# Two of the scan's output additions move from VectorE to ScalarE and TensorE, and the sixteen carry copies of a chunk from GpSimd to ScalarE

## What is computed

```python
dA  = exp(delta[..., None] * A)                   # A: 512 x 16
dBu = (delta * u)[..., None] * B[:, :, None, :]
def step(h, inp):                                 # along the 4096 tokens
    h = dA_t * h + dBu_t
    y_t = einsum('bdn,bn->bd', h, C_t)            # the sum over the 16 states
y = (y + D_skip * u) * silu(z)
out = y @ W_out
```

## Time and profile before

| | |
|---|---|
| median of 3 runs | 2296.16 us (2295.28 to 2297.36) |
| the profiled execution's own time | 2299.68 us |
| its span, first to last instruction | 2297.6 us |
| mean granted TensorE clock | 0.956 of full speed |
| busy: DVE, POOL, PE, ACT | 2096.4, 2039.3, 2053.2, 1696.3 us |
| starts of scan 0 of chunks 7 and 8 | 986.20 and 1121.90 us |

### The profile page before, as it was taken

How to read it: one execution, slowest core, us unless ns; L and a number is a source line. 1 busy time by engine, 2 the same in 40 slices (tenths; PEclk the granted TensorE clock), 3 DMA queues, 4 the chain that set the end, 5 groups by cost and what they waited for, 6 DMA issues and landing times. The chain is left out here.

```text
span 2297.6 us, 30579 instructions
## 1 busy us (share of the span) xinstructions
PE 2053.2 (89%) x9280; PEld 1333.5 (58%) x9280; DVE 2096.4 (91%) x2960; ACT 1696.3 (74%) x2584; POOL 2039.3 (89%) x1657
## 2 busy tenths in 40 slices
PE   7669989899998999999899999999899899987968
PEld 4346565655566565665656556565566656555554
DVE  4999999999999999999999999999999999998940
ACT  5657878787788777787778787878778787875732
POOL 4777999989999998999999999999999999898944
PEclk8759999999999999999999999999999999998989
DMA  5111211112122111112111211211112121111201
GB/s 146 33 33 48 74 56 60 61 52 60 56 68 60 54 61 60 56 56 65 59 58 51 66 60 57 65 60 56 51 60 71 56 61 51 55 58 47 74 19 46
DMA packets 92995, 134.28 MB, mean 58 GB/s; under 512 B 12048, under 2 KB 43024, under 8 KB 92832
## 3 DMA queue, kind: packets, MB, share of 16 engines
q1 hardware_dynamic: 92832, 132.34, 18.6%
HBM read 123.13 MB, written 9.18 MB: 58 GB/s over the span
## 5 line engine op out<-in xcount | busy, mean ns | idle before, releaser
L915 DVE TENSOR_TENSOR_SCAN h<-d_a,carry,d_bu 128x512 f32<-128x512 f32 x1024 | 1258.5, 1268 | 73.4 <-ACT d_a L678 47.0
L1203 POOL TENSOR_TENSOR d_bu<-delta_u,b_rows 128x1024 f32<-128x1024 f32 x512 | 1203.0, 2362 | 4.7 <-issue 0.6
L678 ACT ACTIVATE d_a<-delta,a_neg 128x512 f32<-128x512 f32 x1024 | 694.0, 689 | 425.9 <-DVE h L915 421.3
L495 PE MATMUL ht<-ident,h 128*128 128x128 f32 x4096 | 598.1, 288 | 114.8 <-DVE y_t L930 72.5
L495 PEld LDWEIGHTS ht<-ident,h 128*128 128x128 f32 x4096 | 490.3, 147 | 337.4 <-issue 113.0
L930 DVE SCALAR_TENSOR_TENSOR y_t<-ht,c_t,y_t 128x512 f32<-128x512 f32 x800 | 555.6, 736 | 8.7 <-PE ht L495 8.2
L578 PE MATMUL ring<-x_t,w_gate_sb 128*128 128x512 f32 x640 | 312.1, 617 | 12.8 <-ACT delta L877 10.2
L607 PE MATMUL dn<-w_down_sb,up_hidden 128*128 128x256 f32 x1280 | 305.5, 382 | 6.9 <-ACT c_t L882 4.1
L585 PE MATMUL ring<-x_t,w_up_sb 128*128 128x512 f32 x640 | 294.5, 603 | 16.0 <-ACT silu_gate L809 15.5
L607 PEld LDWEIGHTS dn<-w_down_sb,up_hidden 128*128 128x128 f32 x1280 | 234.6, 190 | 64.3 <-issue 32.5
L1265 POOL TENSOR_TENSOR up_hidden<-silu_gate,up_hidden 128x512 f32<-128x512 f32 x160 | 204.6, 1279 | 51.2 <-ACT up_hidden L815 35.0
(11 more groups left out here) (136 smaller groups left out, 2177.4 us busy)
## 6 DMA issues: line engine op xcount, KB each, us to landing
b_rows<-b_rows_hbm SPq DMA_DIRECT2D x256, 256.0 KB, 3.5
coef_rows<-coef_rows_hbm SPq DMA_DIRECT2D x128, 256.0 KB, 3.4
xa<-L_attn_x_in SPq DMA_DIRECT2D x16, 512.0 KB, 5.0
xr<-L_attn_x_in SPq DMA_DIRECT2D x16, 512.0 KB, 5.0
out<-xr SPq DMA_DIRECT2D x15, 512.0 KB, 2.9
w_in_sb<-L_attn_W_in_in SPq DMA_DIRECT2D x1, 1024.0 KB, 6.3
w_gate_sb<-L_ffn_experts_gate_in SPq DMA_DIRECT2D x2, 512.0 KB, 4.8
w_up_sb<-L_ffn_experts_up_in SPq DMA_DIRECT2D x2, 512.0 KB, 5.5
```

What stands on the lines that cost most here:

```text
L495: last = nc.tensor.transpose(HT[q % HTS][:, j * P:(j + 1) * P], H[:, (NS * c + n) % HS, j, a * P:(a + 1) * P], IDN[:, :])
L678: nc.scalar.activation(DA[i % DAS][:, :], DL[:, r, j, :], ACT.Exp, scale=ANEG[:, j, n:n + 1]).then_inc(ex.sem, 1)
L915: nc.vector.tensor_tensor_scan(H[:, (NS * s + n) % HS, j, :], DA[(n * J + j) % DAS][:, :], BU[:, (2 * n + j // 2) % 4, j % 2, :], CARRY[:, ...
L1203: nc.gpsimd.tensor_tensor(BU[:, (2 * n + h) % 4, :, :], DU[:, 2 * h:2 * h + 2, :], BB[:, n % 2, :].unsqueeze(1).to_broadcast([P, 2, T]), A ...
```

## The change

The pair of slot 46 (q = 40 and 41, quarters 0 and 1 of state 10) is no longer added by DVE. ACT copies it, times C, into `YD[:, 0]` and `YD[:, 1]`, and PE turns it onto y's banks at the chunk's end as it does the held pair: four transposes in slot 63, four in slot 1. All 16 `keep_state` copies of a chunk go from POOL to ACT, at slots written out in `KEEP_ACT` and `KEEP_LAST`, each ahead of that slot's `decay`. `skip_u` is one slot later.

```diff
+        y_kept = [stage(f"y_kept{i}", 2) for i in range(1)]
-        scan, add_c, carry = ..., stage("add_c", (NS - 2) * NT - 6), ...
+        scan, add_c, carry = ..., stage("add_c", (NS - 2) * NT - 8), ...
-        YD_DVE, Y_GATE, OUT_PE = (3, 3, 4, 4), 4, (5, 5, 6, 6)
+        YD_DVE, Y_GATE, OUT_PE = (4, 4, 5, 5), 4, (5, 5, 6, 6)
+        KEEP_ACT = {5: (0,), 12: (1,), 13: (2,), 18: (3,), 20: (4,), 26: (5,), 31: (6,), 37: (7, 8), 41: (9,),
+                    47: (10,), 49: (11,), 59: (12, 13), 63: (14,)}
+        KEEP_LAST = 5
-        SIDE_SLOT, NEXT_SLOT, HELD_SLOT = 20, 26, 56
+        SIDE_SLOT, NEXT_SLOT, HELD_SLOT, YD_SLOTS = 20, 26, 56, (46,)
+        YD_Q = [ADDS[t] for t in YD_SLOTS]
+        ELSEWHERE = SIDE_Q + NEXT_Q + HELD_Q + tuple(q for pair in YD_Q for q in pair)
...
                             if t == 1 and i == 1:
                                 transpose_held(s - 1, (2, 3))
+                                transpose_kept(s - 1, (2, 3))
...
                     if with_scan and t == SLOTS - 1:
                         transpose_y(s, lo, (0, 1), (0, 1))
                         transpose_held(s, (0, 1))
+                        transpose_kept(s, (0, 1))
...
+            def transpose_kept(c, js):
+
+                for i, pair in enumerate(YD_Q):
+                    pe.wait_ge(y_kept[i].sem, y_kept[i].at(c))
+                    for q in pair:
+                        a = q % NT
+                        for j in js:
+                            nc.tensor.matmul(yd_bank(j)[:, a * P:(a + 1) * P],
+                                             YD[:, 2 * i + q - pair[0], j * P:(j + 1) * P], IDN[:, :],
+                                             start=False, stop=False, is_transpose=True, skip_group_check=True)
...
+            def keep_state(c, r, n):
+
+                act.wait_ge(scan.sem, scan.at(c, (n + 1) * J))
+                nc.scalar.activation(CARRY[:, r, n, :], H[:, (NS * c + n) % HS, :, T - 1], ACT.Copy)\
+                  .then_inc(carry.sem, 1)
+
+            def kept_state(c, r, i, q, prepared):
+
+                n, a = q // NT, q % NT
+                act.wait_ge(ht_full.sem, ht_full.at(c, q + 1))
+                act.wait_ge(o_full.sem, o_full.at(c - 1))
+                act.wait_ge(conv_last.sem, conv_last.at(prepared))
+                nc.scalar.activation(YD[:, 2 * i + q - YD_Q[i][0], :], HT[q % HTS][:, :], ACT.Copy,
+                                     scale=CT[:, r, a, n:n + 1]).then_inc(y_kept[i].sem, 1)
...
+                    if ffn and t == KEEP_LAST:
+                        keep_state(s - 1, o, NS - 1)
+                    if with_scan:
+                        for n in KEEP_ACT.get(t, ()):
+                            keep_state(s, r, n)
...
+                    for i, pair in enumerate(YD_Q):
+                        if with_scan and t == YD_SLOTS[i]:
+                            for q in pair:
+                                kept_state(s, r, i, q, s + 1 if prep else s)
...
-                    if t > 0 and t % NT == 0 and with_scan:
-                        keep_state(s, r, n - 1)
...
-                    if t == 0 and ffn:
-                        keep_state(s - 1, o, NS - 1)
...
-            def keep_state(c, r, n):
-
-                pool.wait_ge(scan.sem, scan.at(c, (n + 1) * J))
-                nc.gpsimd.tensor_tensor(CARRY[:, r, n, :], H[:, (NS * c + n) % HS, :, T - 1],
-                                        ONE[:, 0:1].to_broadcast([P, J]), ALU.mult).then_inc(carry.sem, 1)
```

More of the change, by code:

```diff
@@ L167, in mamba_moe_kernel @@
         y_held = stage("y_held", 2)
+        y_kept = [stage(f"y_kept{i}", 2) for i in range(1)]
         stream, tail = stage("stream", 1), stage("tail", NT)
-        scan, add_c, carry = stage("scan", NS * J), stage("add_c", (NS - 2) * NT - 6), stage("carry_s", NS)
+        scan, add_c, carry = stage("scan", NS * J), stage("add_c", (NS - 2) * NT - 8), stage("carry_s", NS)
         stats = {w: stage(f"stats_{w}_s", 2 * NT) for w in ("xa", "o", "x1", "y")}
@@ L239, in added @@
                 return y_held.sem, y_held.at(c, q - HELD_Q[0] + 1)
-            return add_c.sem, add_c.at(c, q - NT + 1 - 2 * ((q > SIDE_Q[1]) + (q > NEXT_Q[1]) + (q > HELD_Q[1])))
+            for i, pair in enumerate(YD_Q):
+                if q in pair:
+                    return y_kept[i].sem, y_kept[i].at(c, q - pair[0] + 1)
+            return add_c.sem, add_c.at(c, q - NT + 1 - sum(q > other for other in ELSEWHERE))
         def gate_slot(f):
@@ L928, in add_state @@
                 else:
-                    dve.wait_ge(*added(c, q - NT if q - NT not in HELD_Q else q - 2 * NT))
+                    apart = q - NT in HELD_Q or any(q - NT in pair for pair in YD_Q)
+                    dve.wait_ge(*added(c, q - 2 * NT if apart else q - NT))
                 nc.vector.scalar_tensor_tensor(YT[:, a, :], HT[q % HTS][:, :], CT[:, r, a, n:n + 1],
@@ L979, in body @@
                     for q in ADDS.get(t, ()):
-                        if with_scan and q >= NT and q not in SIDE_Q + NEXT_Q + HELD_Q:
+                        if with_scan and q >= NT and q not in ELSEWHERE:
                             add_state(s, r, q)
```

## The result

The changed kernel takes 2284.47 us (median of 5, 2284.43 to 2286.68) against 2295.92; the ratio is 0.995 (95% interval 0.9939 to 0.9961). The forecast was 2284.5, range 2272 to 2295. The profiled execution took 2284.43 us, its span 2282.4, so it stands at its median, while the one of before stood 3.5 us above its own.

A forecast was written before the change was run, and what follows sets the result against it. POOL, gapless from slot 45, was taken to set scan 60's start, not the busier DVE. 0.35 - 0.06 + 0.46 + 0 = 0.75 us a steady chunk, 11.7 in all, against the median 2296.16: 2284.5 us, range 2272 to 2295.

The forecast's parts named there:

- POOL, not DVE, sets scan 60: POOL's gapless run from slot 45 sets scan 60's start; 0.61 us gained there out of 1.30 + 0.37.
- the third copy: Slot 56's carry copy: its 0.15 us doesn't help slot 60's additions, so 0.46 remain.
- Chunk 0: No experts there and POOL has room, so DVE's 1.30 us counts whole.
- Scan 42: Three copies (slots 28, 32, 36) leave POOL's run ahead of its d_bu, 0.45 us; its whole 0.35 wait goes.
- A small ACT copy costs 0.06 us: Each of 16 carry copies takes 0.06 us of ACT, bounds 0 and 0.16; only slot 26's lies on a chain.
- The boundary at 0: From one chunk's end to the next, with four transposes before the last state's: net 0, bounds -0.3 and +0.3 us.
- The later skip_u costs 0 and returns 0.15: skip_u one slot later: x_in's delay is covered, cost 0; DVE's idle of 0.15 us ahead of it returns.
- The tail, 0.86: After the last chunk, the eight transposes lie in the open chain and cost 0.86 us.
- The sum: 0.75 us a steady chunk, 14 of them 10.5; 11.7 altogether, 2288.0 from the profiled execution, 2284.5 from the median.
- the first (DVE's time kept whole): POOL gives way more than counted, DVE takes its 1.30 us whole: 24 us, so 2272; chance 0.16.
- the second (the boundary takes it back): Transposes and slot 63's copy hold scans 2 and 3; only scan 42's 0.29 stays: 2291 us; chance 0.20.
- the third: PE's clock drops in slots 4 to 9 behind a larger gap ahead of x_in: slower, up to 2304; chance 0.12.

The follow-up runs named there:

- half_block9: The change with POOL's second product of expert block 9 cut to 4 columns, one routed expert left unweighted; 2267.36 us, ratio 0.9867.
- pair_only: The change with the carry copies (keep_state) left on POOL at their old places; 2297.6 us, ratio 1.0 to the kernel before.
- keeps_only: The kernel before with only the carry copies moved to ACT, DVE's pair and skip_u unchanged; 2292.69 us, ratio 0.9977.
- skip_early: The change with skip_u back in its old slots 3, 3, 4, 4; 2295.88 us, ratio 0.9993 to the kernel before.
- no_turns: The change without its eight PE transposes a chunk, the pair's part of y left out; 2279.22 us, ratio 0.9921.
- block9_late: The change with POOL's two products of expert block 9 in slot 56 instead of 54, its down projection in slot 59 instead of 57; 2280.64 us, ratio 0.9924.
- bank9: The change with block 9's first product on DVE in slot 54, reading up from PSUM, instead of on POOL; 2303.34 us, ratio 1.0034.

## Why the prediction was right, and where not

The forecast of 2284.5 met 2284.47, and its main mechanism held. It is a closer hit than its steps deserve.

 - *POOL, not DVE, sets scan 60.* Right: half_block9 shows it directly, pair_only by what the pair alone is worth. Of DVE's 1.30 us, 0.69 stayed at scan 60 and 0.54 at scan 61; forecast were 0.61 and 0.46. Right too was to leave the third copy out at slot 60's additions: PE's down projection there starts when POOL's product ends, ahead of the third copy, and the additions 4.19 us later, before and after. Chunk 0, where POOL has room, fell by 1.24 us; forecast was 1.30.
 - *Scan 42.* Forecast 0.35 less 0.06 for ACT's copy of slot 26. Measured 0.32, and nothing for the copy: scan 31 did not move.
 - *A small ACT copy costs 0.06 us.* Wrong by size. Timeline of ACT, slots 46 and 47 of chunk 6:

```profile
944.62 1.25 ACT L740 ACTIVATE y_d<-ht,c_t 128x512 f32<-128x512 f32 x2
945.76 0.20 ACT L731 ACTIVATE carry<-h 128x4 f32<-128x4 f32 x1
945.86 1.30 ACT L700 ACTIVATE d_a<-delta,a_neg 128x512 f32<-128x512 f32 x2
```

   The d_a starts 0.10 us after the copy. By an estimate from the figures of the Trainium skill (ScalarE: Activation LUTs, What ACT_TABLE_LOAD costs) 0.19 long and 0.10 apart was to be expected, and the trace agrees (0.20 and 0.10); my row, a copy out of PSUM, was not the nearest after all. It had no weight, since ACT had the room.
 - *The boundary at 0.* The mis-sized term. At half clock the stretch from scan 63 to scan 6 went from 13.33 to 13.44 us on average, at full clock from 13.23 to 12.84; together 0.16 to 0.18 a chunk earlier, inside the stated 0.3. The gain at full clock is the carry copies' doing: keeps_only has 12.86 there.
 - *The later skip_u costs 0 and returns 0.15.* Right that it costs nothing, but the step missed what it is for: with the transposes there, the old slots cost 0.90 us at each half-clock boundary. skip_early shows that it carries some 11 us, nearly the whole gain. Without the transposes, too, it looks to be worth more than 0.15 at half clock: 13.33 us in keeps_only (old slots), 12.92 in no_turns (new ones); no run changes it alone.
 - *The tail, 0.86.* From chunk 15's scan 63 to the end: 98.44 us before, 99.75 after, so 1.3.
 - *The sum.* A chunk fell by 1.04 us in the profiled pair, not 0.75. The 0.29 too little are the boundary (0.18), the pair (0.08 more kept) and scan 42. Against the profiled execution I had 2288.0, and 2284.4 came. Against the median the sum fits, and that is luck, because the profiled execution of before lay 3.5 us above its median and that of after at its own. The medians, 11.45 us apart, ask for about 0.75 a chunk, the two traces for 1.04; which of the recurring waits differ from run to run by those 3.5 us stays open.

Of the rivals, the first (DVE's time kept whole) fell with the wait at scan 60, the second (the boundary takes it back) came about only at half clock and only by 0.11 us a boundary, though no_turns shows that the transposes cost 0.52 there, and the third did not come about: in steady chunks no half-clock stretch fell between scans 3 and 9, although PE's gap ahead of x_in grew from 0.66 to 1.0 us behind a half-clock boundary and from 1.1 to 1.6 behind the others.

## What to carry to other kernels

When two engines run head to head, price a removed instruction at the next place where the other engine is due, not by its own length: here 1.3 us off VectorE were worth nothing until 0.45 us came off GpSimd in the same stretch, and the two together were worth more than their sum. Look for the stretch in which the other engine is gapless and count what leaves or enters that stretch; reordering helped here only up to the end of it (block9_late). A step that seems mere bookkeeping (a consumer moved one slot later) can carry the gain, and a consumer placed one slot too early can lose it (bank9).

## What the runs showed of the hardware

 - A VectorE tensor_tensor with two SBUF inputs took 1.57 and 2.65 us beside GpSimd's d_bu where 0.67 was seen with GpSimd idle; in both it ended 0.55 us after the d_bu. The d_bu itself kept its 2.36 us, and the GpSimd product behind it rose from 1.27 to 1.74. With one input in PSUM the same size took 0.73 to 0.75 beside GpSimd's work.
 - A 128x4 ACT copy out of SBUF takes 0.10 us of ACT's time, a 128x3 one out of PSUM about 0.05.
 - How many of the 14 boundaries run at the 1.2 GHz level changed between kernels with the same PE work there: 7, 3, 9, 1 or 14. It went with PE's idle time in slot 62: none of 13 with 1.2 to 1.5 us, all 13 with 2.7 and 3.2, and anything from few to all in between. A boundary at half clock costs the change 0.60 us.
